# Separate rings for the up and down weights of a mixture-of-experts block, and a new step order, in a four-stage sequence kernel

## What is computed

```python
x = x + _L0_attn_ref(_layernorm(x), ...)   # A: gated linear attention, a scan over time
x = x + _L0_ffn_ref(_layernorm(x), ...)    # B: mixture of 8 experts, top 2, hidden width 352
x = x + _L1_attn_ref(_layernorm(x), ...)   # C: selective scan with 16 states
x = x + _L1_ffn_ref(_layernorm(x), ...)    # D: mixture of 8 experts, top 2, hidden width 128, and 2 shared experts

# one expert, in B and D
h = silu(xt @ w1[e].T) * (xt @ w3[e].T)
y = y + gate_e[:, None] * (h @ w2[e].T)
```

## Time and profile before

| | before |
|---|---|
| median of 3 runs | 2025.4 us |
| lowest, highest | 2016.1, 2026.65 us |
| profiled execution, its own time | 2026.77 us |
| profiled execution, span from first to last instruction | 2025.1 us |
| mean granted TensorE clock | 0.88 |
| DMA traffic | 392.89 MB, mean 194 GB/s |

### The profile page before, as it was taken

How to read it: one execution, slowest core, us unless ns; L and a number is a source line. 1 busy time by engine, 2 the same in 40 slices (tenths; PEclk the granted TensorE clock), 3 DMA queues, 4 the chain that set the end, 5 groups by cost and what they waited for, 6 DMA issues and landing times. The chain is left out here.

```text
span 2025.1 us, 30725 instructions
## 1 busy us (share of the span) xinstructions
PE 1508.2 (74%) x9858; PEld 980.1 (48%) x9858; DVE 1407.6 (70%) x2696; ACT 1111.7 (55%) x2043; POOL 964.3 (48%) x599
## 2 busy tenths in 40 slices
PE   1778888878877668797779877887577768767761
PEld 0234666545645455465545555555355555533540
DVE  3977867778789459778868777789536358679310
ACT  2234363753576377567555666657436656674541
POOL 1032426517336537566166574462736471546464
PEclk8879999989987888898988988999889798888685
DMA  9913556577378567848856488648676688567573
GB/s 249 163 36 95 171 150 175 205 258 226 116 246 261 156 194 273 238 116 250 274 188 148 132 279 299 173 123 269 181 232 184 177 266 294 131 231 236 128 173 63
DMA packets 287833, 392.89 MB, mean 194 GB/s; under 512 B 31640, under 2 KB 225208, under 8 KB 287416
## 3 DMA queue, kind: packets, MB, share of 16 engines
q1 hardware_dynamic: 242616, 357.20, 56.0%
q0 software_dynamic: 45056, 33.72, 9.3%
HBM read 333.10 MB, written 59.69 MB: 194 GB/s over the span
## 5 line engine op out<-in xcount | busy, mean ns | idle before, releaser
L774 POOL DMA_INDIRECT x<-outs,slot_idx x256 | 504.4, 1970 | 467.0 <-DMA outs<-yrow 324.0
L796 PE MATMUL bank<-xT_ring,mix 128*128 128x128 f16 (+1 forms) x1536 | 313.7, 237 | 143.2 <-DMA mix<-weights_B 109.5
L798 PE MATMUL bank<-xT_ring,mix 128*128 128x128 f16 (+1 forms) x1536 | 312.4, 237 | 0.0
L797 PE MATMUL bank<-xT_ring,mix 128*128 128x128 f16 (+1 forms) x1536 | 312.4, 237 | 0.0
L1399 DVE TENSOR_TENSOR_SCAN arena_c<-arena_c 128x1024 f32<-128x1024 f32 x128 | 289.8, 2279 | 5.1 <-ACT arena_c L1132 4.7
L957 PE MATMUL bank<-mix 128*128 128x128 f32 (+1 forms) x1536 | 236.8, 302 | 70.3 <-ACT yrow L1190 34.8
L888 PE MATMUL bank<-arena_c,ident 128*128 128x512 f32 x512 | 264.4, 649 | 19.6 <-DVE arena_c L1385 19.5
L796 PEld LDWEIGHTS bank<-xT_ring,mix 128*128 128x128 f16 (+1 forms) x1536 | 175.4, 114 | 187.6 <-DMA mix<-weights_B 125.9
L957 PEld LDWEIGHTS bank<-mix 128*128 128x128 f32 (+1 forms) x1536 | 210.7, 209 | 113.7 <-DVE mix L1511 63.2
L757 POOL DMA_INDIRECT rows_D<-xrow,slot_idx x128 | 189.0, 1477 | 47.8 <-issue 34.9
L757 POOL DMA_INDIRECT rows_B<-xrow,slot_idx x128 | 173.1, 1352 | 47.1 <-issue 34.0
(11 more groups left out here) (219 smaller groups left out, 2867.1 us busy)
## 6 DMA issues: line engine op xcount, KB each, us to landing
arena_c<-bc_rows SPq DMA_DIRECT2D x256, 512.0 KB, 6.9
mix<-weights_B SPq DMA_DIRECT2D x192, 544.0 KB, 5.0
mix<-weights_D SPq DMA_DIRECT2D x192, 192.0 KB, 3.1
outs<-yrow SPq DMA_DIRECT2D x192, 128.0 KB
xg<-rows_B SPq DMA_DIRECT2D x96, 129.0 KB, 5.5
xg<-rows_D SPq DMA_DIRECT2D x96, 129.0 KB, 3.3
x<-in_x SPq DMA_DIRECT2D x8, 512.0 KB, 4.2
x<-outs,slot_idx POOLq DMA_INDIRECT x256
```

Of the source, the lines that this page charges most:

```text
L774: pool.indirect_dma_start(out=x[:, b % XS, j, :], out_offset=None, in_=y_d[q], in_offset=bass.IndirectOffsetOnAxis(ap=slot_idx[:, q % RJ, ...
L796: pe.matmul(o, hi, xh, start=True, stop=False)
L797: pe.matmul(o, hi, xl, start=False, stop=False)
L798: return pe.matmul(o, lo, xh, start=False, stop=True)
```

## The change

The one ring of whole blocks becomes two rings over all 16 jobs: 2816 words for up weights (two B blocks, or five D blocks) and 1536 words for down weights (two B blocks, or six D blocks); together they take the same 4352 words. `ring` lays the blocks of all jobs one behind the other and notes for each the last earlier block that it overlaps. The transfer of a group is split in two. The up weights (K, `load_up_weights`) wait until the up product `b_c` of the overlapped block has been finished; the down weights (a new letter e, `load_down_weights`) wait until the overlapped block's down product has been finished. There is no other wait at a job's first block than for the table of the job (`placed`). The expert's number is read once and kept in a register for both. TensorE waits for the one in `up_products` and for the other in `down_product`. `ORDER` is another string, with 192 more steps (5771); every letter but e occurs as often as before.

```diff
 ORDER = (
-    "WAAAAAAWAAAAAAAAAWWWWWAAWWAAAAAAAAAAAAAAAWosWWAosAqoAsokkqswwqqAkosAoqsAwkosAwwqoqAoWkAsoqkkksAwowssAoAqqowq"
...
+    "AWAAAWAAWWWACAAWWAAAAAAWWWAAAAAAAWWAAAAAAACCAAAosAoAkCqoAsowAssqqwkokqkswAoAqoAssowkAwkqsowqkqkAossAoqwwsAoq"
...
-    RW = {"B": 2, "D": 5}
...
-        W_WORDS = RW["B"] * NBT * (W13["B"] + W2["B"])
+        PAIR13, PAIR2 = {s: NBT * W13[s] for s in "BD"}, {s: NBT * W2[s] for s in "BD"}
+        RING13, RING2 = 2 * PAIR13["B"], 2 * PAIR2["B"]
+        W_WORDS = RING13 + RING2
+
+        def ring(size, words):
+
+            at, before_it, earlier, start = {}, {}, [], 0
+            for q, (s, _) in enumerate(JOBS):
+                for k in range(BLOCKS):
+                    if start + size[s] > words:
+                        start = 0
+                    end = start + size[s]
+                    over = [key for key, a, b in earlier if a < end and start < b]
+                    at[q, k], before_it[q, k] = start, over[-1] if over else None
+                    earlier.append(((q, k), start, end))
+                    start = end
+            return at, before_it
...
+            "K": [("b_w13", q, k) for q in range(len(JOBS)) for k in range(BLOCKS)],
+            "e": [("b_w2", q, k) for q in range(len(JOBS)) for k in range(BLOCKS)],
...
-            def load_weights(q, k):
-                s = JOBS[q][0]
-                m = block_no[q, k]
-                if k == 0:
-                    wt.wait_ge(s_kept, 16 * (8 + NC["B"] + 2))
-                    wt.wait_ge(placed, q + 1)
-                    if q:
-                        U.wait_filled(wt, "y" + job_before(q))
-                if k >= RW[s]:
-                    U.wait_filled(wt, f"y{q}.{k - RW[s]}")
+            def load_up_weights(q, k):
+                s, m = JOBS[q][0], block_no[q, k]
+                wt.wait_ge(s_kept, 16 * (8 + NC["B"] + 2))
+                wt.wait_ge(placed, q + 1)
+                if before13[q, k]:
+                    U.wait_filled(wt, "c{}.{}".format(*before13[q, k]))
                 for i in range(NBT):
                     e = sp.value_load(table[0:1, q % RJ, NBT * k + i:NBT * k + i + 1], min_val=0, max_val=E - 1)
-                    sp.dma_start(expert_weights(s, k, i),
-                                 Wd[s][bass.ds(e, 1), :, :].rearrange("o p f -> p (o f)")).then_inc(w_in[m % RWL], 16)
+                    expert_of[q, k, i] = e
+                    sp.dma_start(w13_words(q, k, i), Wd[s][bass.ds(e, 1), :, 0:W13[s]].rearrange("o p f -> p (o f)")).then_inc(
+                        w13_in[m % RWL], 16)
+
+            def load_down_weights(q, k):
+                s, m = JOBS[q][0], block_no[q, k]
+                if before2[q, k]:
+                    U.wait_filled(wt, "y{}.{}".format(*before2[q, k]))
+                for i in range(NBT):
+                    e = expert_of.pop((q, k, i))
+                    sp.dma_start(w2_words(q, k, i), Wd[s][bass.ds(e, 1), :, W13[s]:W13[s] + W2[s]].rearrange(
+                        "o p f -> p (o f)")).then_inc(w2_in[m % RWL], 16)
...
             def up_products(q, k, name, parts):
                 s, m = JOBS[q][0], block_no[q, k]
-                wt.wait_ge(w_in[m % RWL], 16 * NBT * (m // RWL + 1))
+                wt.wait_ge(w13_in[m % RWL], 16 * NBT * (m // RWL + 1))
...
             def down_product(q, k):
                 s, n = JOBS[q][0], unit_at["b", (q, k)]
+                m = block_no[q, k]
+                wt.wait_ge(w2_in[m % RWL], 16 * NBT * (m // RWL + 1))
                 U.wait_empty(wt, f"c{q}.{k}")
```

More of the change, by code:

```diff
@@ L81 @@
[L81 to L100, removed]
@@ L128 @@
+    "LKSVYeVNYMOZNYOZUOLSVZNSYOSZSGGGGGGGGGGGGGGGGGG"
 )
@@ L279, in build @@
         xrow16 = xrow[:, :, :].rearrange("p j f -> p (j f)").bitcast(F16).rearrange("p (j f) -> p j f", f=2 * (D + 1))
-        W_WORDS = RW["B"] * NBT * (W13["B"] + W2["B"])
+        PAIR13, PAIR2 = {s: NBT * W13[s] for s in "BD"}, {s: NBT * W2[s] for s in "BD"}
[13 more added lines that the diff above has]
+            return at, before_it
+        at13, before13 = ring(PAIR13, RING13)
+        at2, before2 = ring(PAIR2, RING2)
         U_WORDS = NC["B"] * NB
@@ L295, in build, with w13_words, w2_words, w13 @@
         ysh = y_ring[:, :, :].rearrange("p r n -> p (r n)")
[L297 to L305, removed]
+        def w13_words(q, k, i):
+            n = W13[JOBS[q][0]]
+            return mix2[:, at13[q, k] + i * n:at13[q, k] + (i + 1) * n]
+        def w2_words(q, k, i):
+            n = W2[JOBS[q][0]]
+            return mix2[:, RING13 + at2[q, k] + i * n:RING13 + at2[q, k] + (i + 1) * n]
+        def w13(q, k, i):
+            return w13_words(q, k, i).bitcast(F16).rearrange("p (w f) -> p w f", w=4)
+        def w2(q, k, i):
+            return w2_words(q, k, i).rearrange("p (c d) -> p c d", d=D)
         stage = {}
@@ L413, in build @@
             "a": [st for q in range(len(JOBS)) for st in shared(q, "sh_add", NH)],
-            "K": [("b_weights", q, k) for q in range(len(JOBS)) for k in range(BLOCKS)],
+            "K": [("b_w13", q, k) for q in range(len(JOBS)) for k in range(BLOCKS)],
+            "e": [("b_w2", q, k) for q in range(len(JOBS)) for k in range(BLOCKS)],
             "R": [("b_rows", q, k) for q in range(len(JOBS)) for k in range(BLOCKS)],
@@ L567, in build @@
         silued = sem("silu_parts")
-        w_in = [sem(f"block_weights_{i}") for i in range(RWL)]
+        w13_in = [sem(f"block_up_weights_{i}") for i in range(RWL)]
+        w2_in = [sem(f"block_down_weights_{i}") for i in range(RWL)]
         xg_in = [sem(f"block_rows_{i}") for i in range(RX)]
@@ L944, in up_products @@
                     for j in range(NBT):
-                        wd, rows = w13(s, k, j), slice(j * P, (j + 1) * P)
+                        wd, rows = w13(q, k, j), slice(j * P, (j + 1) * P)
                         last = product(o[:, i * NB + j * P:i * NB + (j + 1) * P], wd[:, v, f], wd[:, v + 1, f],
@@ L956, in down_product @@
                         at = c * NB + j * P
-                        last = pe.matmul(o[:, j * P:(j + 1) * P], w2(s, k, j)[0:rows, c, :], h_ring[n % RH][0:rows, at:at + P],
+                        last = pe.matmul(o[:, j * P:(j + 1) * P], w2(q, k, j)[0:rows, c, :], h_ring[n % RH][0:rows, at:at + P],
                                          start=(c == 0), stop=(c == NC[s] - 1))
```

86 lines of the change are left out of this document (54 added, 32 removed).

## The result

The changed kernel takes 1935.8 us (median; 1926.3 to 1943.1), the kernel before 2025.5 us on the same chip: ratio 0.956 [0.951, 0.962], 4.4% faster. The forecast was 1968, the range 1905 to 2045. The direction and the range held. The gain is 90 us where 57 were forecast. Ratios leave out the few executions that ran in a slower state; the brackets behind a ratio are its 95% interval.

A forecast was written before the change was run, and what follows sets the result against it. No engine is full; PE's waits for B's late up weights (109.5 us) are the largest single loss. From 2026.8 us: -49 early release, -10 clock, +2 second transfer, +3 packets, -5 order, giving 1968 us; range 1905 to 2045.

The forecast's parts named there:

- Size of the problem and of the waits: PE waits 109.5 us for B's up weights, released late; the change should leave 27 us.
- 82 x 0.6 = 49 us: Earlier release of B's up weights removes 82 us of PE wait, of which 0.6 reaches the end: 49 us gained.
- Packing of the order: Heaviest engine per stretch sums to 1581 us before, 1593 after: new string no better packed; all order effects taken as -5 us.
- Clock: PE in the alternating B and D stretch, granted clock 0.90: fewer long waits return some time to 2.4 GHz, 10 us gained.
- Second transfer and smaller packets: 384 more issues on SP, +2 us; rows split into 2816 and 1536 bytes, 49152 more packets, +3 us.
- SP's queue: Letter e's wait for the down product holds next rows and up weights; counted as delaying up weights in 3 of 96 blocks.
- Transfers become the bound: Rival, chance 0.09: B jobs beside stage C reach DMA share about 1, broadcast rows come late; about 2074 us.
- The bound from the D windows: D windows move 255 GB/s per full DMA share; B windows falling to that mix would raise share 0.86 to 1.04.
- The order is unbalanced: Rival, chance 0.11: B2's stretch holds 20 stage C scans instead of 13, DVE work 182 us against 150; about 2039 us.
- More than forecast: Rival, chance 0.16: all 109.5 us of weight waits go and reach the end, clock gives 30; about 1890 us.
- Another wait takes its place: Rival, no change (0.12 with its other form): weights arrive, PE waits at the two up banks instead; about 2028 us.
- the last one: Last 142 us, read as D7 alone: its chain of routing, scatter, 12 blocks and gather stays.

## Why the prediction was right, and where its steps failed

**Size of the problem and of the waits.** The reading that up weights of B came too late for the down product's release was right, and so was the wait of SP for the down product, well under 359 and now 60.7 us. What is left of PE's waits was put at half its size: 27 us were forecast for all of `weights_B`; 30.2 are left at the up product and 24.1 at the down product, 54.3 in all. Stretches of B jobs near 110 us were forecast; B5, B6 and B7 take 108, 87 and 98 from first to last up product. The granted clock of the alternating stretch was 0.92.

**The step that failed: "82 x 0.6 = 49 us".** The prediction gave the early release alone 49 of its net 59 us and called the order no better packed, -5 us with bounds of 0 to +12 and 0 to -24. The runs show otherwise. In the old order the release costs 0.2% [-0.1, +0.4], and taking 90 us of PE's weight waits away is worth nothing: the share that reaches the end is about 0, the lower bound, not 0.6. In the new order the same release takes the time from 1.115 to 0.956. That the forecast landed in its range was in this part luck: its main term brought nothing by itself, and the gain was made by the two edits that it had priced apart. The error was to price them as a sum. An order string is laid out around a buffer's release. In the old one other steps, of DVE above all, stand ahead of what the weights allow, and the trace with K moved up shows PE waiting for them instead. The string fitted to the early release has the next up product ahead of the down product in 76 of 88 pairs and closes the 10.0 us between the old release and the read to 5.1; that this trait carries the gain is not shown.

**Packing of the order.** My sum of the heaviest engine per stretch (1581 before, 1593 after) said that the new string is no better. It counts work, which did not change, and not the idle time between steps that depend on one another, which is where 62 of the 87 us came from. The wrong tool was used for the question. Fewer table loads were right (170 in the trace before, 149 after; 19 forecast from the strings) and ACT's busy time fell by 31 us; what that brings by itself was not tried.

**Clock.** 10 us were forecast. PE's busy time in the alternating stretch fell by 25 us for the same matmuls, with the granted clock at 0.92 for 0.90; since PE and DVE share the gain, no more can be said of its part in the end.

**Second transfer and smaller packets.** +2 and +3 forecast, -7 [-13, -1] measured for both together. The sign was wrong. The likely reason is that the sum counted the shorter landing under the early release only, while the up product waits for less data in the old order too. A cover was named, SP's waiting time, and it held. The packets were more than the 49,152 rows forecast: each of the 384 added transfers also brings 16 packets of 4 bytes, 55,296 in all.

**SP's queue.** "The added wait of SP is the one for the down product; behind it stand the next rows and up weights" was right as a place, but it carried no price. It is the costliest thing tried here: e moved to its release loses 3%, K moved to its release 9% in the old order and 21% in the new. The 24.1 us of new waits for down weights at L993, where "a few us" were forecast, are a miss of their own: e stands far enough back to leave the queue free, and in 11 blocks too far.

**The rivals.** *Transfers become the bound*: the share in B5's stretch rose to 0.97 at 307 GB/s, near the point that I had named, but DVE's waits for broadcast rows fell to 11.2 us, against 33.3 before. It did not decide. The bound from the D windows (255 GB/s per full share) was no ceiling for B windows, which moved 307 / 0.97 = 316. *The order is unbalanced*: not seen; the B jobs are 131 us shorter in sum. *More than forecast*: this is the side on which it came out, though not for its reason, since 54 us of weight waits are left. *Another wait takes its place*: this is what happens in the old order, as the run with K moved up by 4 us shows.

**The middle stretch** gave 7 us back (178 to 185) and the last one nothing (142 in both), as forecast for the last. It isn't D7 alone, though, as the prediction reads it: D6's up products run to 1921 us in the trace before, 38 us into that window.

**Open.** Which trait of the new order carries the gain was not isolated: the one tried, the up product ahead of the down product, was tried with the old ring (slower) and with a clogged SP (hidden), not with rings and a free SP. Nor is it known what the earlier weights would bring in the old order if neither SP's queue nor DVE's order took the time back. The clock's share was not tested apart.

## What to carry to other kernels

Where all engines run one planned order, a buffer's release and the order are one design: price them together, and take a measured wait as the gain only after asking what the planned steps do in that time. Taking the largest wait of the busiest engine away (109.5 to 20 us) gained nothing here. In an in-order DMA queue, put a wait where it is almost met, not where it is first possible: every transfer behind it pays for the lead of the one.

## What was not expected of the hardware

Splitting 192 transfers of 544 KB into 352 and 192 KB, and 192 of 192 KB into 128 and 64, 55,296 more packets, took q1's share from 56.0 to 58.0% and cost no time. The DMA engines held a share of 0.97 at 307 GB/s over 107 us, while DVE waited 11.2 us for broadcast rows in the whole run. And the kernel before took 2018 to 2025 us (medians) beside most of these runs, and 2059 us beside four that ran on another chip (K up by 4 us in the old order, K up and e up in the new, and the new string followed by the old sequence): 1.7 to 2% more, which is larger than the effect of the split or of the release alone, so that only ratios on one chip were compared.
